# Attention and routed experts on one core: loading one block's rows earlier, fetching the first expert's weights ahead, and leaving out TensorE's extra products

## The reference, cut to what matters

```
h = layernorm(x) * (1 + ca) + sa
scores = alpha * tanh(q k / beta) + lam * hamming(h) + lattice(h)      # causal, per head
x = x + ga * (softmax(scores) @ v) @ out_w.T
h = layernorm(x) * (1 + cb) + sb
logits = silu(h @ rw1 + rb1) @ rw2 + rb2                                # 8 experts, best 2 taken
x = x + gb * sum over the two experts of prob * (silu(h @ w1[e] + b1[e]) @ w2[e] + b2[e])
```

## Time and profile before

| what | value |
|---|---|
| median of 3 runs | 1859.3 us (1857.8 to 1864.91) |
| the profiled execution | 1861.52 us |
| its span, first to last instruction | 1859.6 us |
| mean granted TensorE clock | 0.958 of full speed |
| TensorE / VectorE / ScalarE / GpSimd busy | 93% / 70% / 66% / 33% |

### The profile page before, as it was taken

How to read it: one execution, slowest core, us unless ns; L and a number is a source line. 1 busy time by engine, 2 the same in 40 slices (tenths; PEclk the granted TensorE clock), 3 DMA queues, 4 the chain that set the end, 5 groups by cost and what they waited for, 6 DMA issues and landing times. The chain is left out here.

```text
span 1859.6 us, 35364 instructions
## 1 busy us (share of the span) xinstructions
PE 1730.3 (93%) x11140; PEld 1039.0 (56%) x11141; DVE 1309.9 (70%) x2675; ACT 1232.0 (66%) x1260; POOL 620.1 (33%) x715
## 2 busy tenths in 40 slices
PE   4689999999999999999999999899469999999997
PEld 1333434334334344334433334488369999999997
DVE  6457778878888888777877878544646666666664
ACT  1167889999999989989999999633413333333332
POOL 0645241532532553342240201246612222222222
PEclk8878999999999999999999999999779999999998
DMA  4586445667663295336674480272257777777773
GB/s 166 176 197 168 123 135 118 151 131 157 141 132 103 86 197 155 107 98 149 133 159 104 97 196 18 61 230 93 90 195 200 199 199 197 200 199 199 197 201 77
DMA packets 175370, 275.91 MB, mean 148 GB/s; under 512 B 20832, under 2 KB 105952, under 8 KB 173088
## 3 DMA queue, kind: packets, MB, share of 16 engines
q1 hardware_dynamic: 159904, 252.34, 50.6%
q0 software_dynamic: 13440, 17.97, 5.7%
q10 hardware_dynamic: 1920, 4.23, 0.7%
HBM read 205.51 MB, written 68.96 MB: 148 GB/s over the span
## 5 line engine op out<-in xcount | busy, mean ns | idle before, releaser
L1341 DVE SCALAR_TENSOR_TENSOR probs<-probs,scal,bil_ps 128x512 f32<-128x512 f32 (+1 forms) x1152 | 789.6, 715 | 237.8 <-PE bil_ps L1183 193.3
L1262 ACT ACTIVATE probs<-probs 128x2048 f32<-128x2048 f32 (+1 forms) x288 | 522.5, 1814 | 80.8 <-DVE probs L1341 80.1
L1255 ACT ACTIVATE probs<-raw_ps 128x2048 f32<-128x2048 f32 (+1 forms) x288 | 509.3, 1768 | 31.5 <-PE raw_ps L1165 22.7
L1183 PE MATMUL bil_ps<-u_mv,w_st 50*128 50x512 f32 (+3 forms) x1280 | 468.0, 454 | 28.7 <-DVE probs L1341 17.1
L1183 PEld LDWEIGHTS bil_ps<-u_mv,w_st 50*128 50x128 f32 x1280 | 198.9, 187 | 511.5 <-DVE probs L1341 424.9
L2063 ACT ACTIVATE rows_sb<-fc_ps,b 128x128 f32<-128x128 f32 x576 | 161.0, 369 | 345.3 <-DVE hid_lo L2095 304.5
L1202 PE MATMUL o_ps<-probs,v_sb 128*32 128x512 f32 (+3 forms) x2560 | 299.8, 550 | 2.7 <-POOL probs L1012 2.6
L1165 PE MATMUL raw_ps<-q_mv,k_st 64*128 64x512 f32 (+3 forms) x1280 | 270.1, 394 | 6.5 <-DMA q_mv<-q_split 4.7
L2019 PE MATMUL fc_ps<-modrow,rows_sb 128*128 128x128 f32 x2304 | 270.9, 276 | 0.0
L2019 PEld LDWEIGHTS fc_ps<-modrow,rows_sb 128*128 128x128 f32 x2304 | 264.9, 193 | 0.0
L1992 POOL DMA_INDIRECT out<-modrow,token x72 | 125.4, 1741 | 379.1 <-DVE modrow L2128 373.4
(11 more groups left out here) (233 smaller groups left out, 1531.6 us busy)
## 6 DMA issues: line engine op xcount, KB each, us to landing
rows_sb<-in_w SPq DMA_DIRECT2D x72, 1024.0 KB, 4.9
q_mv<-q_split SPq DMA_DIRECT2D x128, 128.0 KB, 5.5
rows<-x_rows SPq DMA_DIRECT2D x72, 130.0 KB, 2.1
v_rows<-rows_sb SPq DMA_DIRECT2D x8, 1024.0 KB, 6.1
o_t<-o_sb SPq DMA_DIRECT2D x32, 256.0 KB, 6.6
k_st<-k_split SPq DMA_DIRECT2D x16, 512.0 KB, 8.3
k_st<-k_split SPq DMA_DIRECT2D x32, 256.0 KB, 10.8
v_sb<-v_rows SPq DMA_DIRECT2D x8, 1024.0 KB, 14.0
```

The source lines that it names most:

```text
L1183: mm = pe.matmul(bil_ps[:, hd % 2, column:column + width], codes(kt)[row:row + BIAS_ROWS, :], u_mv[row:row + BIAS_ROWS, p, hd // 2, query: ...
L1255: act.activation(probs[:, s % NBUF, :, first:BLK], raw_ps[:, :, first:BLK], ACT.Tanh).then_inc(tanh_ready, 1)
L1262: act.activation(scores, scores, ACT.Exp).then_inc(exp_ready, 1)
L1341: dve.scalar_tensor_tensor(scores, scores, scal[:, ALPHA:ALPHA + 1], bil_ps[:, hd % 2, first:BLK], ALU.mult, ALU.add).then_inc(sum_ready, 1)
```

## The change

It has four parts.

1. `FILL_AT` and `keep_clock` go: in the 145 steps that have no entry in `SLOT`, TensorE issues nothing between the first and the second bilinear product of step s+3.
2. `load_rows(2)` is issued by SyncE ahead of its first store instead of after the loads of iteration 0.
3. The `w1` of the first tile is loaded by SyncE at the end of the router stage, once the first two blocks are scattered (they count on a semaphore of their own), the tile's expert is known and GpSimd has issued all scatters (`all_sent`); tile 0's step in the expert stage loads its rows only.
4. Of the low halves of `w2`, the one for expert 4 leaves the loop, those for 4, 1, 2 and 7 come at the end and only after `all_sent`, and those for 5 and 6 are made by VectorE in the steps of tiles 0 and 1 of the expert stage; `w2_raw` keeps its place for them. TensorE waits for them (`w2_low`) ahead of its first second product.

```diff
-FILL_AT = {}
-for s in range(NSTEP):
-    if s not in SLOT:
-        last = max(n for n in SLOT if n < s)
-        i, o, half = SLOT[last][-1]
-        assert half != 0
-        FILL_AT[s] = (i, o)
...
+            load_rows(2)
             for o in ("Q0", "Q1", "C", "L"):
                 store(0, o)
...
             load_values(0)
-            load_rows(2)
             load_keys(1)
...
-            def keep_clock(part):
-
-                i, o = part
-                if o == "C":
-                    pe.matmul(part_ps[ROWS:P, :], ident[:, ROWS:P], modrow[:, 0:BLK], start=True, stop=True)
-                else:
-                    pe.wait_ge(emptied, EMPTIED[i, o])
-                    pe.matmul(part_ps[:, :], ident[:, :], modrow[:, 0:BLK], start=True, stop=True)
-
...
                 for i, o, half in SLOT.get(s, []):
                     project(i, o, half)
-                if s in FILL_AT:
-                    keep_clock(FILL_AT[s])
                 if s + PE_LEAD < NSTEP:
                     bilinear(s + PE_LEAD, (1,))
...
+            sp.wait_ge(pads_ready, 2)
+            sp.wait_ge(tr_mm, 2)
+            sp.wait_ge(first_scattered, 16 * 2 * SLOTS)
+            sp.wait_ge(all_sent, 1)
+            e = sp.value_load(tile_expert[0:1, 0:1], min_val=0, max_val=E - 1)
+            src = a["w1"].rearrange("e (k p) n -> e p k n", p=P)[ds(e, 1), :, :, :]
+            sp.dma_start(rows_sb[:, 0:KC * HID].rearrange("p (k n) -> p k n", k=KC),
+                         src.rearrange("z p k n -> (z p) k n")).then_inc(w1_first, 16)
...
-                                                rows_sb[:, tile * PAY:(tile + 1) * PAY], None).then_inc(scattered, 16)
+                                                rows_sb[:, tile * PAY:(tile + 1) * PAY], None
+                                                ).then_inc(first_scattered if n < 2 else scattered, 16)
...
             for n in range(1, N_RBLK):
                 scatter(n)
-            pool.wait_ge(scattered, 16 * NTILE * TOPK)
+            pool.sem_inc(all_sent, 1)
+            pool.wait_ge(first_scattered, 16 * 2 * SLOTS)
+            pool.wait_ge(scattered, 16 * (N_RBLK - 2) * SLOTS)
...
-                    for i, e in enumerate((0, 3, 4)):
+                    for i, e in enumerate((0, 3)):
...
-            dve.tensor_copy(tile_expert[:, :], expert_f[:, :])
+            dve.tensor_copy(tile_expert[:, :], expert_f[:, :]).then_inc(pads_ready, 1)
...
-            for i, e in enumerate((1, 2, 7, 5, 6)):
-                dve.wait_ge(w2_hi_ready, 3 + i + 1)
+            dve.wait_ge(all_sent, 1)
+            dve.wait_ge(w2_hi_ready, E)
+            for e in (4, 1, 2, 7):
                 low_half(e)
...
                     sp.dma_start(rows[:, u % 2, :], dram["x_rows"][ds(row, P), :]).then_inc(rows_in[u % 2], 16)
+                    if isinstance(m, int) and m == 0:
+                        return
...
                         pe.wait_ge(w2_in, 16 * (E + 1))
+                        pe.wait_ge(w2_low, 2)
...
+                    if isinstance(m, int) and m < 2:
+                        part = ds((5 + m) * W2E, W2E)
+                        dve.tensor_tensor(w2_split[:, 1, part], w2_raw[:, part], w2_split[:, 0, part].bitcast(F32),
+                                          ALU.subtract).then_inc(w2_low, 1)
```

More of the change, by code:

```diff
@@ L315, in build @@
             pass
-        with nc.sbuf_tensor("w2_place", [P, E * HID // P * D], F32, side="right"):
+        with nc.sbuf_tensor("w2_raw", [P, E * HID // P * D], F32, side="right") as w2_raw:
             with nc.sbuf_tensor("rw1_hi", [P, KC * HID], F32R, side="right") as rw1_hi:
@@ L336, in build @@
                             rw1_hi, rw1_lo, x1_stored, h2_back, out)
[L337 to L340, removed]
+            w2_low = ctx.enter_context(nc.semaphore("w2_low"))
+            w1_first = ctx.enter_context(nc.semaphore("w1_first"))
+            stage_router(nc, a, dram, modrow, ident, rows_sb, w2_raw, w2_split, w2_in, out, wo, den, ln, rw1_hi, rw1_lo,
+                         tile_expert, expert_f, tile_row, x1_stored, h2_back, w1_first)
+        stage_experts(nc, a, dram, modrow, ident, rows_sb, tile_expert, expert_f, tile_row, w2_raw, w2_split, w2_in, w2_low,
+                      w1_first, out)
 HAM, SCALE, ALPHA, BETA, SIG_HAM, SIG_SCALE, HALF_LAM, LAT_SCALE, INV_BETA, ROOM = range(10)
@@ L1419, in skewed, with stage_router @@
         emit(m, m, lambda k: 0 <= m - k < total)
-def stage_router(nc, a, dram, modrow, ident, rows_sb, w2_split, w2_in, out, wo, den, ln, rw1_hi, rw1_lo,
-                 tile_expert, expert_f, tile_row, x1_stored, h2_back):
+def stage_router(nc, a, dram, modrow, ident, rows_sb, w2_raw, w2_split, w2_in, out, wo, den, ln, rw1_hi, rw1_lo,
+                 tile_expert, expert_f, tile_row, x1_stored, h2_back, w1_first):
     with ExitStack() as ctx:
@@ L1434, in stage_router @@
         right = lambda n, s, dt=F32: ctx.enter_context(nc.sbuf_tensor(n, s, dt, side="right"))
-        w2_raw = right("w2_raw", [P, E * HID // P * D])
+        right("w2_place", [P, E * HID // P * D])
         right("rw1_place", [P, KC * HID])
@@ L1442, in stage_router @@
         normed = inv_w.rearrange("p k (z d) -> p (k z) d", d=D)
-        w2_hi_ready, w2_lo_ready = sem("w2_hi_ready"), sem("w2_lo_ready")
+        w2_hi_ready, first_scattered, all_sent = sem("w2_hi_ready"), sem("first_scattered"), sem("all_sent")
         w2_part = lambda e: ds(e * HC * D, HC * D)
@@ L1749, in low_half @@
                 dve.tensor_tensor(w2_split[:, 1, w2_part(e)], w2_raw[:, w2_part(e)],
-                                  w2_split[:, 0, w2_part(e)].bitcast(F32), ALU.subtract).then_inc(w2_lo_ready, 1)
+                                  w2_split[:, 0, w2_part(e)].bitcast(F32), ALU.subtract)
             def split_rows(n):
@@ L1950, in stage_experts @@
         rows_in = [sem(f"rows_in{p}") for p in range(2)]
-        w1_in = [sem(f"w1_in{p}") for p in range(WB)]
+        w1_in = [w1_first] + [sem(f"w1_in{p}") for p in range(1, WB)]
         b1_in = sem("b1_in")
@@ L1980, in step @@
                                  ).then_inc(w1_in[u % WB], 16)
-            skewed(sp, NET, 0, UNROLL, step)
+            skewed(sp, NET, 1, UNROLL, step)
         @block.gpsimd
```

4 lines of the change are left out of this document (2 added, 2 removed).

## The result

| what | before | after |
|---|---|---|
| median | 1861.06 us (5 runs, 1857.8 to 1864.91) | 1913.91 us (1905.02 to 1953.66) |
| ratio, with 95% interval | | 1.0291 [1.023, 1.0353] |
| the profiled execution: time / span | 1861.52 / 1859.6 us | 1932.5 / 1930.7 us |
| its mean granted clock | 0.958 | 0.889 |
| stretches of half clock in attention | 5, 37.6 us in all | 30, 318.6 us in all |

The ratio compares the means of the runs, without the one of 1953.66 us, which counts as slow. The profiled execution after lies 19 us above its median. All that follows from it about sizes is from that one execution; the medians say +53 us.

What follows compares the result with a forecast made beforehand. ScalarE was taken to pace attention wherever TensorE keeps its clock. Terms: 42 - 4 - 4 - 4.2 - 4.1 - 3.7 = +22 us on the profiled 1861.5, so 1883.5, median about 1881; range 1842 to 1922.

Steps and rivals of the forecast that it cites:

- The bound and the mechanism: Attention: ScalarE sets the pace at full clock; TensorE's clock falls where a short last step's products stand nearly alone.
- 20 new falls: Attention without the extra products: the clock falls to half at 16 more iteration ends, plus four falls in bare full steps.
- four falls: Attention: the new clock falls added for bare full steps, 68 of the last 76 steps having no piece.
- I take 2.1: Attention: price in us of one bare clock fall, between 1.0 and 2.4; 20 of them make +42 us.
- The third rival: Attention: bare full steps cannot bring the clock back, each taking about 4.5 us; about 1939 us, chance 0.08.
- The first rival: Attention: short steps without a piece keep the clock; part 1 gives -6, all parts -18, 1841 us; chance 0.20.
- Gain 4 us at full clock: Attention: the bilinear product starts some 0.2 us earlier without the extra product; 4 us taken, between nothing and 28.
- -4.2 us: Head of attention: earlier rows end TensorE's 3.1 us wait for mask 0, query load issued 1.1 earlier; between 0 and -8.
- -4.1 us: Router's end: the next stage begins at 1352.4 instead of 1356.58; +1.3 if the lag hangs on VectorE, -6 if scatters decide.
- with VectorE held back by `all_sent`: Router's end: the last four scatters take 5 us instead of 9.4, as VectorE's low halves wait.
- the later of GpSimd's end plus 7.3 and VectorE's end plus 0.4: Router's end: the rule for when the next stage begins, the later of 1350.4 and 1352.4.
- -3.7 us: Experts' start: with tile 0's w1 in place, the first product comes about 6.7 us after the boundary, not 10.4; -6 to 0.

Runs made afterwards that it cites:

- e6_twelve_rows: The changed kernel with an extra product put back in the same 145 steps, reading 12 rows instead of 128; 1943.5 us (one run).
- e7_ends_only: The changed kernel with the full extra product put back only in the last and last but one step of an iteration, 27 of 145; 1851.8 us (one run).
- e2_no_extra: The kernel before without the 145 extra products and with nothing else changed; 1923.9 us, ratio 1.035 to the kernel before.
- e1_put_back: The changed kernel with the 145 extra products put back, so parts 2, 3 and 4 alone; 1849.8 us, ratio 0.9964 to the kernel before.
- e5_held_back: e1_put_back with GpSimd raising all_sent by a one-column memset behind its last scatter instead of a bare semaphore increment; 1847.8 us (one run).

## Why the prediction was right, and where it was not

Slower was forecast at 0.60, by the clock, and it came so, inside the range; the centre was 33 us short. That the forecast's own range of 1857 to 1915 just holds 1913.9 is partly luck: its upper end does not follow from its terms, since 28 falls of 2.4 are 67 us, which gives 1906 with the other parts as forecast and 1926 with them at nothing. By its own steps:

- **The bound and the mechanism: right.** I had read it from the pieces in front of the falls, L with 6 rows and the half of G with 12; e6_twelve_rows shows that an extra product of 12 rows does not hold the clock either. The reading that "elsewhere" it held was too neat: at step 169 the clock fell with a full extra product in the step before, and a fall at step 151 came in most later traces.
- **"20 new falls": 25 in the profiled execution.** The list of places was fair: at 11 of the 16 ends named a fall begins within two steps, and with the end products alone missing there were 11 new ones. The step that failed is that I costed the places one by one and gave the bare full steps "four falls". That is what they cause alone (e7_ends_only), but bare steps and bare ends together make more falls than either makes alone, and longer ones.
- **"I take 2.1" for a fall: 75.1 / 25 = 3.0.** At an end by itself it was 2.1 (23.1 us for 11). The rest is length: 47 and 41 us at half clock in single stretches, where the four of before after the start had 3.4 to 6.8. A bare full step at half clock takes 5.07 us, where I took 4.5 by leaving the product's whole time out of 6.90. It costs 1.5 us more than at full clock.
- **The third rival, "the half clock lasts", happened in part.** It was priced at 1939 for all bare steps. In the last 76 steps the clock was lost and regained many times, with two long stretches. Its 0.08 was too little; the one stretch that came back in 6.9 us had pieces behind it, so it said nothing about bare steps.
- **The first rival, that the clock holds, fell.** e2_no_extra alone rules it out. (Its "-6" for part 1 should be -8 by its own terms, -4 and -4.)
- **"Gain 4 us at full clock": not separable.** Bare steps that lie at full clock take 3.67 us on average instead of 3.71, which would be 6 us for 145; in e7_ends_only it is of the size of the falls that came with it.
- **Part 2, "-4.2 us": the waits went as forecast, the size is not separable.** GpSimd's wait for the rows and TensorE's for mask 0 are gone. e1_put_back has exactly 4.2 at steps 9 to 14, but that is partly luck: the other traces with the products in place have from -4.7 to +2.9 at step 14, by when the clock rises and falls in the head. In the changed kernel 9.4 us at step 3 shrink to 2.3 at step 12 through the fall at 125.2.
- **The boundary, "-4.1 us": -0.7.** The step that failed is "with VectorE held back by `all_sent`": the bare increment passed the queued scatters. Once it was mended, "the later of GpSimd's end plus 7.3 and VectorE's end plus 0.4" gave the boundary to 0.1 us (1345.61 + 0.33): 3.0 us under e1_put_back, and 4.0 under the kernel before, where -4.1 was forecast.
- **The experts' start, "-3.7 us": -2.3,** and 2.0 over the stage. The first product starts 8.09 us after the boundary, not 6.7. Both low halves hid, the first beside the first product.

Parts 2 to 4 were forecast at -12 and measured -6.7; part 1 at +34 and measured +64 to +65.

What stays open: why a stretch appears at steps 24, 38, 169 or 182 in one execution and not in another with the same attention code, why the one at step 151 stays, and whether the narrow product is cheaper by more than its 0.1 us.

## What to carry to other kernels

A product whose result nobody reads may be what keeps TensorE's clock up. Before taking such products out, look at which products stand in front of the falls that the trace already has. TensorE's busy share told nothing about it here, and two products of nearly one duration differed in it. Price the places together and not one by one: where the steps between them are bare too, the clock fell more often here and came back later. If they cost something, keep them at the short steps, make them as narrow and short as still works, and put none beside a step where the clock never fell.

A semaphore that is to say "all is sent" must be raised by an instruction that takes its turn behind the sends, and the trace shows at once whether it was: look at what starts before the last send ends.

## What the runs showed of the hardware that I had not expected

- Two products of nearly equal duration, 12 rows by 128 columns (median 692 ns for one matmul) and 128 rows by 12 columns (596 ns; at least 587 and 592), did the opposite to the clock: 29 stretches of half clock against 4.
- TensorE shown busy for 84% of 41 and of 47 us stayed at half clock all that time (changed kernel).
- A bare semaphore increment on GpSimd took effect while at least five indirect DMAs issued before it were still waiting to run (2.60 us and on); a 0.12 us memset behind them did not pass them.
- While VectorE made low halves, a scatter on GpSimd took 1.89 to 2.60 us; with VectorE waiting (e5_held_back) the same scatters took 0.96 us.
- Between executions of the same attention code the half clock comes and goes at the same few places: e1_put_back has it at 209.7 and 264.3 us and e5_held_back at 671.4, 743.1 and 801.1. Of the changed kernel, the four runs that enter the ratio took 1905 to 1932.5 us with mean clocks from 0.911 down to 0.889, and the longer ones have the lower clock.
